# An attention and mixture-of-experts kernel on one core: VectorE's layer norm laid over other units of the iteration

## The reference, cut to what matters

```python
xn = _layernorm(x, axis=-1)                    # x: (16, 512, 256)
key_mask = jnp.sign(jnp.abs(jnp.sum(xn, axis=-1)))       # also the query mask
Q, K, V = relu(xn @ Wq + bq), relu(xn @ Wk + bk), relu(xn @ Wv + bv)   # 16 heads of 16
scores = where(key_mask == 0 or above the diagonal, NEG, Q @ K.T / sqrt(16))
attn = softmax(scores) * query_mask
attention = layernorm(attn @ V + xn) * gamma + beta
logits = xn @ router_w.T + experts_bias        # top 2 of 8 experts
x = x + attention + experts(xn) + shared_expert(xn)
```

## Time and profile before

| what | value |
| --- | --- |
| median of 3 runs | 2275.74 us (2273.53 to 2276.35) |
| the profiled execution's own time | 2274.43 us |
| its span, first to last instruction | 2272.5 us |
| TensorE clock granted, mean share | 0.938 |
| PE busy | 1920.2 us (84%) |
| DVE busy | 1397.2 us (61%) |
| ACT busy | 1080.1 us (48%) |
| POOL busy | 1121.6 us (49%) |

### The profile page before, as it was taken

One profiled execution on the slowest core, in us unless ns is written; L12 is line 12 of the kernel. 1 busy time (PEld: TensorE's weight loads), 2 busy tenths in 40 slices (PEclk: granted clock), 3 DMA queues, 4 the chain that ended last, 5 costly groups with the idle time before them and its releaser, 6 DMA issues. The chain is left out here.

```text
span 2272.5 us, 37245 instructions
## 1 busy us (share of the span) xinstructions
PE 1920.2 (84%) x13238; PEld 1377.9 (61%) x13238; DVE 1397.2 (61%) x2934; ACT 1080.1 (48%) x2048; POOL 1121.6 (49%) x935
## 2 busy tenths in 40 slices
PE   0478887888898888889766999999999999799997
PEld 0235544444454444445325888888888888577776
DVE  6577787777777777876513465555556543355554
ACT  0125554454455555445444666666666665222221
POOL 5444443444544354452233677776867753533331
PEclk9679999998999999899878999999999999899998
DMA  1664566566556556655335566566666653544441
GB/s 35 121 104 77 104 114 117 122 124 128 113 112 125 119 121 118 123 118 117 88 133 173 185 210 211 186 203 201 213 210 199 211 159 101 165 132 123 129 130 56
DMA packets 235375, 314.01 MB, mean 138 GB/s; under 512 B 18971, under 2 KB 200357, under 8 KB 229029
## 3 DMA queue, kind: packets, MB, share of 16 engines
q1 hardware_dynamic: 222948, 278.63, 47.8%
q0 software_dynamic: 12288, 33.57, 5.8%
HBM read 211.43 MB, written 100.70 MB: 137 GB/s over the span
## 5 line engine op out<-in xcount | busy, mean ns | idle before, releaser
L482 ACT ACTIVATE pT<-st_ps 128x512 f32<-128x512 f32 (+1 forms) x704 | 384.3, 561 | 518.3 <-PE st_ps L982 366.5
L1625 PE MATMUL gu<-xc,w_up_h 128*128 128x512 f32 x1760 | 555.3, 397 | 40.7 <-DVE hf L1515 19.6
L706 DVE TENSOR_REDUCE mx<-s_ps 128x1 f32<-128x512 f32 (+3 forms) x704 | 439.2, 639 | 208.3 <-PE s_ps L961 139.2
L959 PE MATMUL s_ps<-k_aug,q_aug 97*128 97x512 bf16 (+3 forms) x1024 | 295.6, 321 | 132.2 <-DVE mx L706 107.1
L1625 PEld LDWEIGHTS gu<-xc,w_up_h 128*128 128x128 f32 x1760 | 324.7, 190 | 129.0 <-issue 34.4
L1625 PE MATMUL gu<-xc,w_up_l 128*128 128x512 f32 x880 | 345.4, 392 | 2.1 <-issue 2.1
L980 PE MATMUL st_ps<-q_aug,k_aug 99*128 99x512 bf16 (+3 forms) x1024 | 290.9, 317 | 56.0 <-ACT pT L482 36.1
L1347 POOL TENSOR_TENSOR w_up_l<-w_raw,w_up_h 128x512 fp32r<-128x512 f32 x160 | 203.9, 1296 | 210.1 <-ACT w_up_h L1429 210.1
L1515 DVE TENSOR_TENSOR hf<-sil,gu 128x512 f32<-128x512 f32 x220 | 151.0, 687 | 234.0 <-ACT sil L1434 233.4
L959 PEld LDWEIGHTS s_ps<-k_aug,q_aug 97*128 97x128 bf16 x1024 | 100.8, 100 | 315.0 <-DVE mx L706 219.7
L1639 PE MATMUL yp<-w_dn_h,hid_h 128*128 128x256 f32 x880 | 254.7, 289 | 18.9 <-DVE hid_l L1517 18.9
(11 more groups left out here) (206 smaller groups left out, 3538.9 us busy)
## 6 DMA issues: line engine op xcount, KB each, us to landing
w_raw<-in_L_ffn_w_dram SPq DMA_DIRECT2D x117, 512.0 KB, 6.2
part_scr<-parts SPq DMA_DIRECT2D x64, 384.0 KB, 4.2
q_aug<-part_scr SPq DMA_DIRECT2D x192, 128.0 KB
k_aug<-part_scr SPq DMA_DIRECT2D x192, 128.0 KB
xr<-expert_rows SPq DMA_DIRECT2D x39, 512.0 KB
expert_results<-yo SPq DMA_DIRECT2D x39, 512.0 KB, 3.3
x_sb<-in_L_attn_x_dram SPq DMA_DIRECT2D x16, 512.0 KB, 4.9
layernorm_rows<-xn SPq DMA_DIRECT2D x16, 512.0 KB, 3.4
```

Source lines behind the costliest of these rows:

```text
L482: fn(pT[:, j % 2, h:h + heads, 0:w], unit_view(st_ps[u % 2], heads, w), ACT.Exp).then_inc(exp_done, 1)
L706: vec.tensor_reduce(mx[:, q, h:h + heads], unit_view(s_ps[u % 2], heads, keys), AX_X, ALU.max).then_inc(s_max, 2)
L959: mm(v[:, n], q_aug[par][0:ROWS_S, h0 + n, P * q:P * (q + 1)], k_aug[par][0:ROWS_S, h0 + n, 0:keys], start=True, stop=False)
L1625: last = mm(gu[m % 2][:, a], w_up[wpar][x][:, a, c, P * m:P * (m + 1)], xc[par][:, y, c], start=k == 0, stop=k == 3 * NC - 1)
```

## The change

The numbers in AT_NORM, AT_MASK, AT_MASKS, AT_SQUARE and AT_BEST are units.

- The masks of a batch are no longer made at the end of the iteration that normalises it (units 41 and 42), but in the next one, in units 13, 14 and 16, in tiles of their own (`mlanes`, `mtree`, `msum`). PE transposes them at unit 20 and no longer at 13.
- The row sums of the next batch are made in units 35 and 37, and no longer in units 1 and 2 of the iteration that goes on with them. Those of batches 0 and 1 come in iteration -3.
- The mean is subtracted in unit 2 (was 3), the squares summed in 11 and 12 (were 14 and 15), the quotient's first product made in 25 (was 24) and its bits cut in 27 (was 26).
- The transposes of xn and its store wait for `normed`, POOL's last instruction, and no longer for the masks.
- The choice of experts, in iterations 2, 6 and 10, stands in units 0, 1, 3, 30, 31 and 33 (were 4, 6, 9, 10, 12 and 16). Ranks and slots stay in 36, 38 and 39.

```diff
-        AT_MASK = 13
+        AT_MASK = 20
-        AT_SQUARE = 9
+        AT_SQUARE = 8
-        AT_NORM = (1, 2, 3, 14, 15, 18, 20, 24, 26, 41, 42)
+        AT_NORM = (35, 37, 2, 11, 12, 18, 20, 25, 27)
+        AT_MASKS = (13, 14, 16)
-        AT_BEST = (4, 6, 9, 10, 12, 16)
+        AT_BEST = (0, 1, 3, 30, 31, 33)
...
             def store_norm(b):
-                await_(sp, xn_ready, b + 1)
+                await_(sp, normed, b + 1)
...
             def ln_centre(b):
                 ln(vec.tensor_scalar(sm[:, MEAN], sm[:, SUM], 1.0 / C, None, ALU.mult))
+                await_(dve, normed, b)
...
             def ln_masks(b):
+                mask_begin(b)
                 await_(dve, normed, b + 1)
-                ln(vec.tensor_reduce(lanes[:], xn[:].rearrange("p t (k l) -> p t l k", l=16), AX_X, ALU.add))
+                mask(vec.tensor_reduce(mlanes[:], xn[:].rearrange("p t (k l) -> p t l k", l=16), AX_X, ALU.add))
+
+            def ln_masks_fold(b):
+                v, t1, t2 = (x[:].rearrange("p t (a b) -> p t a b", b=w) for x, w in ((mlanes, 4), (mtree1, 4), (mtree2, 2)))
+                mask(vec.tensor_tensor(t1[:, :, 0], v[:, :, 0], v[:, :, 1], ALU.add))
+                mask(vec.tensor_tensor(t1[:, :, 1], v[:, :, 2], v[:, :, 3], ALU.add))
+                mask(vec.tensor_tensor(mtree2[:], t1[:, :, 0], t1[:, :, 1], ALU.add))
+                mask(vec.tensor_tensor(mtree3[:], t2[:, :, :, 0], t2[:, :, :, 1], ALU.add))
+                mask(vec.tensor_tensor(msum[:], mtree3[:, :, 0], mtree3[:, :, 1], ALU.add))
...
+                    if i == -3 and s == 0:
+                        ln_mean(0)
+                        ln_mean_fold(0)
                     if norm:
-                        if s == AT_NORM[0]:
-                            ln_mean(i + 3)
-                        if s == AT_NORM[1]:
-                            ln_mean_fold(i + 3)
...
+                    if 0 <= i + 4 < B:
+                        if s == AT_NORM[0]:
+                            ln_mean(i + 4)
+                        if s == AT_NORM[1]:
+                            ln_mean_fold(i + 4)
+                    if project:
+                        if s == AT_MASKS[0]:
+                            ln_masks(i + 2)
...
             def mask_rows(b):
+                await_(pe, mk_ready, b + 1)
...
                         if s == AT_X[0]:
-                            await_(pe, xn_ready, b + 1)
+                            await_(pe, normed, b + 1)
```

More of the change, by code:

```diff
@@ L123, in attention_phase @@
         sm = sb("sm", [P, 20, NT])
+        mlanes, msum = sb("mlanes", [P, NT, 16]), sb("msum", [P, NT])
+        mtree1, mtree2, mtree3 = sb("mtree1", [P, NT, 8]), sb("mtree2", [P, NT, 4]), sb("mtree3", [P, NT, 2])
         msk, mq = sb("msk", [P, NT]), sb("mq", [P, B, NT])
@@ L669, in ln_quotient_bits @@
                                   ).then_inc(q_ready, 1)
+            mask_begin, mask_mark, mask, mask_end = chain(dve, chain_mask, 9)
             def ln_masks(b):
+                mask_begin(b)
                 await_(dve, normed, b + 1)
-                ln(vec.tensor_reduce(lanes[:], xn[:].rearrange("p t (k l) -> p t l k", l=16), AX_X, ALU.add))
+                mask(vec.tensor_reduce(mlanes[:], xn[:].rearrange("p t (k l) -> p t l k", l=16), AX_X, ALU.add))
[6 more added lines that the diff above has]
+                mask(vec.tensor_tensor(msum[:], mtree3[:, :, 0], mtree3[:, :, 1], ALU.add))
             def ln_masks_end(b):
-                fold(lanes[:], sm[:, SUM], ln)
-                ln(vec.tensor_scalar(msk[:], sm[:, SUM], 0.0, None, ALU.not_equal))
+                mask(vec.tensor_scalar(msk[:], msum[:], 0.0, None, ALU.not_equal))
                 await_(dve, mk_ps, b)
-                ln_mark(vec.tensor_scalar(mq[:, b], msk[:], 0.0, INFINITE, ALU.is_equal, ALU.mult))
-                ln_mark(vec.tensor_scalar(mk[:, 0], msk[:], 1.0, None, ALU.mult))
-                vec.tensor_scalar(mk[:, 1], msk[:], 1.0, -MASKED, ALU.subtract, ALU.mult).then_inc(xn_ready, 1)
+                mask_mark(vec.tensor_scalar(mq[:, b], msk[:], 0.0, INFINITE, ALU.is_equal, ALU.mult))
+                mask_mark(vec.tensor_scalar(mk[:, 0], msk[:], 1.0, None, ALU.mult))
+                vec.tensor_scalar(mk[:, 1], msk[:], 1.0, -MASKED, ALU.subtract, ALU.mult).then_inc(mk_ready, 1)
             def x_low(b, c):
@@ L895, in body @@
                             ln_quotient_bits(i + 3)
[L896 to L899, removed]
                             ln_end()
+                    if 0 <= i + 4 < B:
[6 more added lines that the diff above has]
+                            ln_masks(i + 2)
+                        if s == AT_MASKS[1]:
+                            ln_masks_fold(i + 2)
+                        if s == AT_MASKS[2]:
+                            ln_masks_end(i + 2)
+                            mask_end()
                 if maxima:
@@ L1045, in body @@
                         if s == AT_MASK:
-                            await_(pe, qf_ready, 2 * NC * b + 1)
+                            await_(pe, qf_ready, 2 * NC * b + 4)
                             mask_rows(b)
@@ L1051, in body @@
                         if s == AT_K[3]:
-                            await_(pe, mk_out, b + 1)
+                            await_(pe, qf_ready, 2 * NC * b + 1)
                             project_tile(b, 3)
@@ L1062, in body @@
                         if project:
-                            await_(pe, qf_ready, 2 * NC * b + 4)
+                            await_(pe, mk_out, b + 1)
                         await_(pe, neg_out[1], i + 1)
```

10 lines of the change are left out of this document (5 added, 5 removed).

## The result

The changed kernel takes 2332.57 us (2329.51 to 2333.99, 4 runs), the kernel before beside it 2276.05: ratio 1.0251, interval 1.0238 to 1.0264. The forecast of 2294 had the sign and a third of the size; the time lies outside the range.

What follows compares the result with a forecast made beforehand. Bound: a loop closed by the scatter, where only release to q_ready counts. Terms 11.2 (ordinary iterations) + 12.0 (routing) + 2.4 (no scatter) - 6.8 (start) = +18.8 on 2274.4 gives 2293.2, median 2294; range 2256 to 2305.

Steps and rivals of the forecast that it cites:

- The loop: Iterations with a scatter: release, units 1 to 26, q_ready, 13.2 us quotient, 10.1 us scatter, 1.7 us; only release to q_ready can change.
- Tail 0: Masks leaving units 41 and 42, row sums entering 35 and 37: behind q_ready, covered by the scatter wait, 0.
- Rival 2: Freed ends shorten the loop: the release follows DVE and PE done sooner at unit 43; 2237 us, chance 0.12.
- A: Start of an ordinary iteration: row sums leave units 1 and 2, -0.7 us (bounds 0 and -1.8).
- B: Units 11 to 20: 3.4 us of new work, partly in idle time, plus held adds; +1.5 us (-1.7 to +2.4).
- some 2.7 lie where the new work can use them: Units 11 to 20: of 3.7 us DVE idle time, 2.7 usable by the 3.4 us of new work, leaving +0.7.
- one of L640 and L641 goes free: Units 11 to 20: one of two adds held by POOL's instructions is no longer held, returning 0.9 us.
- C: At q_ready: bits cut one unit later, so one more row maximum lies before them; +0.6 us.
- Routing: Iterations 2, 6 and 10: second-pass picks and row sums under the quotient delay slots and scatter by +4.0 us each, +12.0.
- Iterations -1 to 2 and the end: Iterations -1, 0 and 1, without a scatter: A and B count, C does not; +0.8 us each, +2.4.
- Start: Early transposes move everything behind by 3.6 us; first row maximum at 94.5 instead of 101.25, -6.8 us.
- Rival 4: Worse: B at its high bound, and held adds delay PE by more than their own time; 2306 and above, chance 0.06.

## Why the prediction was right in sign and wrong in size

The ten iterations 3 to 12, from the end of one scatter to the end of the tenth behind it, cut at the starts of DVE's row maxima and of POOL's quotient. Each number is the sum over ten, in us, read from the traces (the 667.9 of the earlier trace rows end at DVE's start and not at the scatter's end):

| stretch | before | changed | masks in 13, 14, 16 alone | row sums alone | masks in 9, 10, 16 alone |
| --- | --- | --- | --- | --- | --- |
| scatter's end to unit 8 | 125.4 | 122.8 | 120.5 | 131.4 | 120.1 |
| units 9 and 10 | 46.1 | 46.3 | 46.7 | 46.2 | 49.3 |
| units 11 to 20 | 178.7 | 214.8 | 210.4 | 178.5 | 175.0 |
| unit 21 to the quotient's start | 77.4 | 82.0 | 76.0 | 76.5 | 76.6 |
| quotient's start to scatter's end | 239.9 | 247.1 | 241.0 | 243.0 | 241.5 |
| all | 667.6 | 713.0 | 694.7 | 675.7 | 662.5 |

Units 11 to 20 carry 36.1 of the 45.4 us, and the masks alone put 31.7 there. The masks alone and the row sums alone make 27 and 8 of the whole. No run moves the sum of squares or the cut bits alone.

- **The loop: right, where the boundary is held.** An iteration grew by what was laid between the release and q_ready. *Tail 0* held: in an ordinary iteration units 27 to 40 grew from 14.2 to 18.3 us (the first add of the row sums is held for 2.22 us), 2.8 us of units 41 and 42 were freed, and neither shows in the period, since DVE waits 5.05 us for the scatter. Rival 2, that freed ends shorten the loop, had its place where nothing holds: on the chip with 2166 us, with one-input adds, moving the masks added 27.9 us in units 11 to 20 over iterations 3 to 11 and gave 25.7 back in units 41 and 42, and the nine grew by 3.8 (567.6 against 563.8). The masks cost the same 3 us there; what differs is whether the freed units pay.
- **A: right.** 11.10 us became 10.09 in the row above (forecast -0.7, bounds 0 and -1.8). What lies between the scatter's end and unit 1 grew from 1.7 to 2.2 us, as DVE now stands one or two units earlier in its order.
- **B: the step that failed.** Forecast +1.5, upper bound +2.4; measured 22.13 - 17.88 = +4.25 (in the iterations that route and those behind them +2.7; +3.6 in the mean of ten). The lock is not the error: freeing the adds of the three sums gives only 0.7 back here, and without any of them held the stretch still grows by 2.9, where "That leaves +0.7" was forecast. The error is in "some 2.7 lie where the new work can use them". With the masks alone the idle time before the second cast stays in front of it (1.20 us) with the sum behind it, and PE waits 2.23 us for the next row maximum, 0.27 before. In the changed kernel the sum of squares fills that idle time, PE waits 3.7, and DVE's wait comes back at unit 17. The masks alone cost this with no add held, and nothing in 9 and 10, which rules out both the lock and the work as such. The second cast did come free (0.42 us, 1.37 before), but "one of L640 and L641 goes free" did not hold in sum: the multiplication (L640 before, L644 now) is at 0.16 us, the add behind it is still held, and the scaling behind that, free before, is held now. DVE, then POOL:

```profile
744.18 1.11 DVE L645 TENSOR_TENSOR sm<-sm 128x4 f32<-128x4 f32 x1
745.32 1.09 DVE L646 TENSOR_SCALAR sm<-sm 128x4 f32<-128x4 f32 x1
745.23 1.16 POOL L427 TENSOR_TENSOR parts<-r,parts 128x512 bf16<-128x512 f32 x1
```

  The scaling is a `tensor_scalar` with one input. The Trainium skill ("SBUF — State Buffer", Who interferes with whom) counts it among the operations that can take the shared ports when their operands meet certain conditions. The trace agrees: it ends with POOL's L427 (746.41 and 746.39).
- **C: right.** From unit 21 to the quotient it is 8.17 us in the row above, and was 7.84 (655.30 to 663.14 in the earlier trace rows): +0.3 here, +0.5 in the median iteration, forecast +0.6.
- **Routing: right in size.** An iteration that routes grew by 10.1 us and the one behind it by 1.3, so the pair grew by 3.0 more than two others; the forecast's +4.0 beside +1.4 means 2.6. The scatter comes 7.5 us after the quotient ("5 us or more"), 5.6 later than before, where 4.0 were forecast. The row sums alone account for 2.6 of them. The picks are behind the other 3.0, and their run puts what they cost at 5 us for three such iterations or less.
- **Iterations -1 to 2 and the end: a term left out.** Forecast +2.4 and +4.0 up to the first scatter's end, measured +12.1. Iterations -1, 0 and 1 grew by 8.4 us (190.7 against 182.3) and not by 2.4: B again, and the row sums. The sum counts only A and B there, though no scatter's wait covers what stands behind q_ready. In iterations 0 and 1 units 35 to 37, with an add held for 2.22 us, take 6.5 us and not 2.0, and the freed units 41 and 42 give 1.4 back. The +9.9 behind the last boundary was forecast at nothing. Some 6 of it lie before the end of the next scatter, where iteration 13 still makes masks (units 11 to 20 take 17.57 us, 13.78 before), and some 4 behind the last scatter, in the second phase; that was not taken apart.
- **Start: right in kind, partly by luck.** Forecast -6.8, measured -9.9. That "all behind them moves by 3.6" does not follow from the early transposes: with the waits alone they start at 54.03 us, as here, and the quotient of batch 1 still starts at 84.69 and not at 81.2. In the changed kernel it starts at 80.46. The held adds ended at 91.2 and not at 94.3, since the last of them was held only by POOL's last instruction but one. Rival 4 (2306 and above, 0.06) named the side on which the time fell. Of its two reasons, B went past its high bound of +2.4, but for sums that nothing holds; that "a held add delays PE by more than its own time" was not what decided.

## What to carry to other kernels

Idle time absorbs new work only if it stands behind that work in the engine's own order. Before laying work into a stretch, ask what each wait in it is for, and put the work ahead of the wait. A wait for another engine that is itself full (units 9 and 10) takes it free; a wait that another engine ends for its own reasons, with the new work behind it, passes the whole length on. And where an iteration is closed by something outside (here the hold), work freed behind the last deadline buys nothing; where it is not, in the first iterations or on a chip without the hold, the same freed units paid some 2.8 us an iteration in kernels with the masks moved alone.

## What the runs showed of the hardware

While POOL's eight indirect transfers run, PE's results reach DVE and ACT late. On the chips where the kernel before takes 2273 to 2280 us, DVE's waits for them at a boundary are 0.4 to 6.5 us long, and the last one ends 1.4 to 1.9 us after the scatter at most boundaries. With the same 10 us of scatter, in four traces of a chip where the kernel before takes 2166, none of DVE's waits at the boundaries into iterations 3 to 13 is over 0.8 us, but for one boundary (1.63 and 1.23 us). With all eight in front of the quotient the first long wait comes 4 to 6 us after the first transfer. In two halves the kernel gains 27 us, and with the masks out of units 41 and 42 it gains 42; four transfers in a row held between nothing and 2.4 us, depending on the place and the kernel. TensorE's clock goes with it: granted 0.92 over ten iterations where PE's results are held and it then idles, 0.97 with the halves, 0.98 where they are not held. Which is cause and which effect, and what on the chip holds the results, stays open; no run here separates a chip's clock from its holds.

A VectorE add with two inputs in SBUF (0.17 us alone) took up to 2.24 us beside POOL's instructions on 128x1024, and the same sum written as a reduction with one input was never held.
